# A first layer norm left out and block turns taken off TensorE, in a two-stage token kernel

## The chip, the cores and the metric

One core of a Trainium2 chip runs the whole kernel. The metric is the time of one execution on the device in microseconds; the median of 3 runs is shown. A core has TensorE (PE), VectorE (DVE), ScalarE (ACT), GpSimd (POOL) and SyncE (SP), each with its own instruction stream; they wait for each other by semaphores. DMAs are issued by SyncE here, and at the start by GpSimd too.

## What is computed

```python
# x: 8192 tokens of 512; all matrices are 512x512, all numbers float32
weights = AB/sqrt(512) * exp(W @ (ab*G).T - 0.5*|W|^2 * ab^2)     # random features of the weights
feats   = AB/sqrt(512) * exp(x @ (ab*G).T - 0.5*|x|^2 * ab^2)     # and of the tokens
x = layernorm(x + feats @ weights.T)                              # first norm
real, imag = x @ cos(theta + theta_noise), x @ sin(phi + phi_noise)
x = layernorm(x + sqrt(real**2 + imag**2))                        # second norm
```

## The kernel before

The tokens are worked in NB = 16 blocks of B = 512, each as C = 4 tiles of 128 tokens. Products are in float32 split into a rounded part (`_hi`) and a rest (`_lo`): three matmuls of 128x128 by 512 columns for each.

A block b goes through these steps on TensorE: the mix of features with weights (L813 to L815, 48 matmuls, into `token_ps[0..3]`), the projection of block b + 2 (L761 to L763, 48 matmuls, four results), the turns (L824: each tile of 128x512 as 4 transposes of 128x128 against the identity, into `turn_ps`), and the second stage. That is plain for blocks 0 and 1 (`PLAIN` = 2) and from block 2 on one level of a Winograd scheme: the tiles are taken in two pairs, a pair's turned features are halves, seven products M1 to M7 of six matmuls each are made (L910 to L912), and VectorE joins them (`join_u` and so on, L1375 to L1405). The order is M1, M6, M7, M5, M2, M4, M3. M1 needs only a first half, M6 needs the half sums.

Around it, for each tile: VectorE adds x to the mix (`residual1`, L1138), takes its statistics (L1109, L1113), GpSimd makes 1/sqrt(var + eps) and -mean times it (`scale1`, L377 to L393, four instructions on one column), ScalarE applies the first norm (`norm1`, L646), TensorE turns the tile, ScalarE rounds the turned tile out of PSUM (L651, L656, L657), VectorE makes the rest (L1015) and the half sums (L1354 to L1359), ScalarE rounds those (L661) and VectorE makes their rest (L1015). After the products ScalarE squares the joined tiles (L671), GpSimd adds the two squares of a pair (`pair_sum`, L398), ScalarE takes the root (L586), GpSimd or VectorE adds the residual (L402, L1334), VectorE takes the statistics (L1164), GpSimd the scales (`pair_scale2`, L408 to L414), ScalarE applies the second norm (`norm2`, L592) and SyncE stores a tile (L264). The norm of a block's last pair runs inside the next block's step.

For the block after next VectorE makes the exponents out of the projection's banks (L1020, `project_ps`, two banks used in turn), ScalarE the features (L503, L504), VectorE their rest (L1015); ScalarE rounds the turned input xT (L531) and VectorE splits it (`split_columns`, L1015, two instructions of 128x1024). The tokens' norms go through ScalarE (L462), a VectorE transpose (L1101), DRAM and back (L249, L253).

Each engine's order is written out by hand; each works strictly in that order, also SyncE, so that a wait in it holds up all DMAs behind it. The start makes cosine and sine on GpSimd, VectorE and ScalarE and waits for them in places. The last block has an order of its own.

## Time and profile before

| | us |
|---|---|
| median of 3 runs (lowest, highest) | 727.46 (727.32, 727.57) |
| the profiled execution, whole | 727.33 |
| its span in the profile | 725.5 |
| TensorE busy | 708.5 |
| VectorE busy | 563.8 |
| ScalarE busy | 489.7 |
| GpSimd busy | 279.2 |

Times of rows are microseconds from the start of the span; "busy" leaves out waits and the issue of DMAs. In a row of the timeline the first number is the start, the second the length, and the brackets at the end tell how long the engine had stood idle and what released it.

### The profile page before, as it was taken

What the parts mean: (1) busy time and instruction counts of PE and PEld (TensorE: products, weight loads), DVE (VectorE), ACT (ScalarE), POOL (GpSimd) and SP (SyncE); (2) the same over time, 40 slices, a digit from 0 to 9 for tenths busy, and PEclk for the clock granted to TensorE, in tenths of its full rate; (3) what the DMA queues carried; (4) which work ended last, traced back from release to release, by engine and by line L of the source; (5) the groups of instructions that cost most, each with busy time, mean ns of one, the idle gap of its engine ahead of it and who ended that gap; (6) DMA issues with size and microseconds to landing.
All of it is one profiled execution on the core that took longest, in us unless ns stands there. A gap on an engine that the chain in (4) does not pass through costs nothing.

```text
span 725.5 us, 10937 instructions
## 1 busy us (share of the span) xinstructions
PE 708.5 (98%) x3228; PEld 582.8 (80%) x3228; DVE 563.8 (78%) x963; ACT 489.7 (68%) x760; POOL 279.2 (38%) x465
## 2 busy tenths in 40 slices
PE   8999999999999999999999999999999999999993
PEld 7876788888888888888888888888888888888872
DVE  5799789797777868778786877869687777877686
ACT  7746757584957769395775939677594867757463
POOL 5765026606144250614416062341605235160525
PEclk9999999999999999999999999999999999999998
DMA  8761032310403232050322205032130503200011
GB/s 301 221 136 54 15 115 69 122 59 27 162 15 118 70 106 67 15 173 15 116 72 81 92 15 173 15 116 72 61 113 15 171 17 116 70 32 29 1 58 58
DMA packets 32753, 60.80 MB, mean 84 GB/s; under 512 B 3168, under 2 KB 3168, under 8 KB 32736
## 3 DMA queue, kind: packets, MB, share of 16 engines
q1 hardware_dynamic: 31584, 58.50, 24.3%
q0 software_dynamic: 1152, 2.10, 1.7%
q8 instruction: 8, 0.13, 0.1%
q14 instruction: 9, 0.07, 0.0%
HBM read 43.78 MB, written 16.81 MB: 84 GB/s over the span
## 4 chain that ended last, share of the span: by engine, by line
PE 90%; DVE 5%; ACT 2%; POOL 1%; issue 1%; POOLq 0%; ACTq 0%; DVEq 0%
PE token_ps L910 9%; PE token_ps L912 9%; PE token_ps L911 9%; PE token_ps L815 8%; PE token_ps L813 8%; PE token_ps L814 7%; PE project_ps L763 7%; PE project_ps L761 7%; PE project_ps L762 7%; PE turn_ps L824 4%; PE project_ps L910 3%; PE project_ps L912 3%; PE project_ps L911 3%; PE token_ps L843 1%; PE token_ps L841 1%; PE token_ps L842 1%
## 5 line engine op out<-in xcount | busy, mean ns | idle before, releaser
L398 POOL TENSOR_TENSOR late<-late 128x1024 f32<-128x1024 f32 x29 | 71.6, 2470 | 306.7 <-ACT late L671 306.7
L761 PE MATMUL project_ps<-xT_hi,gs_hi 128*128 128x512 f32 x248 | 100.1, 404 | 0.0
L813 PE MATMUL token_ps<-W_hi,F_hi 128*128 128x512 f32 x256 | 99.7, 389 | 0.0
L815 PE MATMUL token_ps<-W_hi,F_lo 128*128 128x512 f32 x256 | 99.6, 389 | 0.0
L814 PE MATMUL token_ps<-W_lo,F_hi 128*128 128x512 f32 x256 | 99.6, 389 | 0.0
L763 PE MATMUL project_ps<-xT_hi,gs_lo 128*128 128x512 f32 x248 | 97.1, 392 | 0.0
L762 PE MATMUL project_ps<-xT_lo,gs_hi 128*128 128x512 f32 x248 | 96.7, 390 | 0.0
L586 ACT ACTIVATE late<-late 128x1024 f32<-128x1024 f32 x29 | 30.8, 1062 | 77.1 <-POOL late L398 77.1
L671 ACT ACTIVATE late<-late 128x1024 f32<-128x1024 f32 x54 | 57.2, 1059 | 33.1 <-DVE late L1400 28.8
L646 ACT ACTIVATE z<-z,shift,rstd 128x512 f32<-128x512 f32 x56 | 45.2, 808 | 40.0 <-POOL shift L393 40.0
L1138 DVE TENSOR_TENSOR z<-token_ps,x_tok 128x512 f32<-128x512 f32 x64 | 44.1, 689 | 30.9 <-PE token_ps L815 27.6
L910 PE MATMUL token_ps<-T_hi,zT_hi 128*128 128x512 f32 x168 | 65.6, 390 | 0.0
L912 PE MATMUL token_ps<-T_hi,zT_lo 128*128 128x512 f32 x168 | 65.4, 389 | 0.0
L911 PE MATMUL token_ps<-T_lo,zT_hi 128*128 128x512 f32 x168 | 65.4, 389 | 0.0
L1015 DVE TENSOR_TENSOR zT_lo<-turn_ps,zT_hi 128x512 fp32r<-128x512 f32 x64 | 35.2, 568 | 33.1 <-ACT zT_hi L651 27.4
L1020 DVE SCALAR_TENSOR_TENSOR expo<-norm_bc,neg_half_ab,project_ps 128x512 f32<-128x512 f32 x62 | 46.0, 742 | 17.8 <-PE project_ps L763 16.0
L814 PEld LDWEIGHTS token_ps<-W_lo,F_hi 128*128 128x128 f32 x256 | 48.1, 188 | 10.0
L815 PEld LDWEIGHTS token_ps<-W_hi,F_lo 128*128 128x128 f32 x256 | 48.0, 188 | 10.0
L813 PEld LDWEIGHTS token_ps<-W_hi,F_hi 128*128 128x128 f32 x256 | 48.0, 188 | 9.9
L763 PEld LDWEIGHTS project_ps<-xT_hi,gs_lo 128*128 128x128 f32 x248 | 46.5, 188 | 10.2
L762 PEld LDWEIGHTS project_ps<-xT_lo,gs_hi 128*128 128x128 f32 x248 | 46.7, 188 | 9.1 <-issue 0.2
L761 PEld LDWEIGHTS project_ps<-xT_hi,gs_hi 128*128 128x128 f32 x248 | 46.6, 188 | 9.2 <-DVE xT_lo L1015 0.2
(214 smaller groups left out, 1802.7 us busy)
## 6 DMA issues: line engine op xcount, KB each, us to landing
x_tok<-in_x SPq DMA_DIRECT2D x16, 1024.0 KB, 5.6
out_tokens<-o_tile SPq DMA_DIRECT2D x62, 256.0 KB, 2.2
plain_xT_lo<-in_xT SPq DMA_DIRECT2D x14, 1024.0 KB, 5.3
norm_bc<-token_norms SPq DMA_DIRECT2D x15, 256.0 KB, 3.0
plain_T_hi<-in_gsT SPq DMA_DIRECT2D x4, 256.0 KB, 4.3
z<-in_wT SPq DMA_DIRECT2D x4, 256.0 KB, 4.6
plain_T_lo<-in_xT SPq DMA_DIRECT2D x1, 1024.0 KB, 7.9
plain_T_hi<-in_theta SPq DMA_DIRECT2D x4, 256.0 KB, 6.5
```

The costliest lines, as they stand in the source:

```text
L398: pool.tensor_tensor(parts[:, p, :, 0, :], parts[:, p, :, 0, :], parts[:, p, :, 1, :], ALU.add).then_inc(sum_made, 2)
L671: nc.scalar.activation(parts[:, p, i, :, :], parts[:, p, i, :, :], ACT.Square).then_inc(square_done, 2)
L761: nc.tensor.matmul(o, gs_hi[:, c, cols], rhs_hi[:, c, :], start=(c == 0), stop=False)
L762: nc.tensor.matmul(o, gs_hi[:, c, cols], rhs_lo[:, c, :], start=False, stop=False)
L763: return nc.tensor.matmul(o, gs_lo[:, c, cols], rhs_hi[:, c, :], start=False, stop=(c == C - 1))
L813: nc.tensor.matmul(o, F_hi[:, c, cols], W_hi[:, c, :], start=(c == 0), stop=False)
L814: nc.tensor.matmul(o, F_hi[:, c, cols], W_lo[:, c, :], start=False, stop=False)
L815: return nc.tensor.matmul(o, F_lo[:, c, cols], W_hi[:, c, :], start=False, stop=(c == C - 1))
L910: nc.tensor.matmul(o, left[0][i], right[0][i], start=(i == 0), stop=False)
L911: nc.tensor.matmul(o, left[0][i], right[1][i], start=False, stop=False)
L912: last = nc.tensor.matmul(o, left[1][i], right[0][i], start=False, stop=(i == H - 1))
L1020: stt(out=expo[:, to, :], in0=norm_bc[:, k, :], scalar=neg_half_ab[:, j:j + 1], in1=bank[:, :], op0=ALU.mult, op1=ALU.add).then_inc(expo_m ...
```

## The change

From block 1 on the first norm is left out. What it did is put elsewhere: the mean over features is taken out by subtracting from each row of cos and sin its column's mean (once, in the second block's step), and the scale by adding to the second norm's variance `damp` = eps * (var + eps) in place of eps. The residual that goes on is z without its norm.

From block 2 to 14 TensorE doesn't turn tiles. VectorE transposes a pair (128x1024) in squares of 32x32, SyncE stores it in 4 DMAs to DRAM in runs of 32 numbers (128 B) and fetches it in 3 DMAs (256, 128 and 128 KB, in runs of 128 numbers) to where the halves are wanted in SBUF. The half sums and rounding read that. The freed banks `turn_ps` take projections 2 and 3, so the projections wait for no exponent. The splits of xT go from VectorE to GpSimd. The last block keeps TensorE's turns, of the tiles without norm.

```diff
@@ build(), tensors
+    turned_dram = [nc.dram_tensor(f"turned_pair_{p}", (2 * D, P), F32, kind="Internal").ap() for p in range(2)]
-        parts = late.rearrange("p (q i t) d -> p q i t d", q=2, i=2)
+        parts = late.rearrange("p (q t i) d -> p q i t d", q=2, i=2)
+        turned_squares = [late[:, 4 * p + 2:4 * p + 4] for p in range(2)]
+        chunk_sums = [late[:, 0:2], late[:, 2:4]]
+        column_means = [late[:, 1, :], late[:, 3, :]]
@@ SyncE
+            def store_squares(b, p):
+                sp.wait_ge(squares_turned, 2 * (b - PLAIN) + p + 1)
+                rows = turned_dram[p].rearrange("(k r) (a t) -> a r k t", r=32, t=32)
+                for a in range(P // 32):
+                    src = turned_squares[p][32 * a:32 * a + 32].rearrange("r i (k t) -> r (i k) t", t=32)
+                    sp.dma_start(rows[a], src).then_inc(squares_stored[p], 16)
+            def fetch_halves(b, p):
+                sp.wait_ge(squares_stored[p], 64 * (b - PLAIN + 1))
+                first, second = turned_dram[p].rearrange("(i c q) n -> i q c n", i=2, q=P)
+                place = lambda lo, hi: zT_raw[:, p, lo * Q:hi * Q].rearrange("q (c n) -> q c n", n=P)
+                sp.dma_start(place(0, 2), first).then_inc(halves_landed[p], 16)
+                sp.dma_start(place(6, 7), second[:, 0:H]).then_inc(halves_landed[p], 16)
+                sp.dma_start(place(2, 3), second[:, H:C]).then_inc(halves_landed[p], 16)
...
                 if not first:
                     store_out(b - 1, 0)
                     store_out(b - 1, 1)
+                if moved:
+                    store_squares(b, 0)
+                    fetch_halves(b, 0)
+                    store_squares(b, 1)
+                if not first:
+                    store_out(b - 1, 2)
+                    store_out(b - 1, 3)
                 if ahead:
                     sp.wait_ge(y_made, C * (b + 1))
                     sp.dma_start(x_tok[:, slot], x_blocks[b + 2]).then_inc(x_loaded[slot], 16)
-                if not first:
-                    store_out(b - 1, 2)
-                    store_out(b - 1, 3)
+                if moved:
+                    fetch_halves(b, 1)
@@ GpSimd
-            def scale1(b, j):
...
+            def sum_chunks(k, raw):
+                pool.wait_ge(sine_made, 4 * C)
+                pool.tensor_tensor(chunk_sums[k], raw[:, 0:H, :], raw[:, H:C, :], ALU.add).then_inc(chunk_sums_made, 1)
...
+            def centre(k, raw, parts_made):
+                pool.wait_ge(parts_made, C)
+                pool.wait_ge(mean_copied, k + 1)
+                for c in range(C):
+                    pool.tensor_tensor(raw[:, c, :], raw[:, c, :], column_means[k], ALU.subtract).then_inc(centred, 1)
...
+            def step(b, ahead):
                 pair_sum(b - 1, 1)
-                scale1(b, 0)
                 pair_scale2(b - 1, 0)
-                scale1(b, 1)
                 pair_scale2(b - 1, 1)
-                scale1(b, 2)
-                scale1(b, 3)
+                make_damp(b)
+                if ahead:
+                    split_columns(b + 2, 0)
+                    split_columns(b + 2, 1)
                 pair_sum(b, 0)
                 pair_residual2(b, 0)
@@ ScalarE, step of a block
-                def norm1(j):
...
+                def round_halves(p):
+                    act.wait_ge(halves_landed[p], 48 * (s + 1))
+                    nc.scalar.activation(zT_hi[:, p, 0:3 * Q], zT_raw[:, p, 0:3 * Q], ACT.Copy).then_inc(halves_hi_made, 1)
@@ TensorE
+                    if j < 2:
+                        pe.wait_ge(chunk_sums_made, 2 * (j + 1))
+                        nc.tensor.matmul(turn_ps[j][:, :], ones[:, :], chunk_sums[j][:, 0, :],
+                                         start=True, stop=True).then_inc(mean_done, 1)
...
                     for j in range(C):
-                        pe.wait_ge(expo_made, C * (b + 2) + j - 1)
-                        project(j, project_ps[j % 2])
-                        if j < 2:
-                            turn(b, j)
-                    turn(b, 2)
-                    turn(b, 3)
+                        project(j, wide_project_ps[j])
@@ VectorE
+                def turn_squares(p):
+                    both = slice(2 * p, 2 * p + 2)
+                    dve.wait_ge(y_made, C * b + 2 * p + 2)
+                    nc.vector.transpose(turned_squares[p], z[:, both, :]).then_inc(squares_turned, 1)
+                def split_halves(p):
+                    dve.wait_ge(halves_hi_made, 2 * s + p + 1)
+                    dve.wait_ge(half_sums_made, 8 * s + 4 * p + 4)
+                    lower(zT_lo[:, p, 0:3 * Q], zT_raw[:, p, 0:3 * Q], zT_hi[:, p, 0:3 * Q]).then_inc(halves_lo_made, 1)
...
                 residual1(b, slot, 1)
+                moments1(0)
                 if more:
+                    turn_squares(0)
+                    pair_residual2(b - 1, 1)
...
+                    residual1(b, slot, 3)
+                    moments1(1)
+                    turn_squares(1)
...
+                    next_exponent(b, slot, 1, wide_project_ps)
+                    landed_half_sums(0)
+                    split_halves(0)
+                    next_exponent(b, slot, 2, wide_project_ps)
+                    split_half_sums(0)
+                    split_feature_pair(C * (b + 2) + 1, 0)
+                    next_exponent(b, slot, 3, wide_project_ps)
+                    landed_half_sums(1)
+                    join_u(0)
+                    split_halves(1)
+                    join_v(0)
+                    join_c22(0)
+                    join_w(0)
+                    join_c11(0)
+                    split_half_sums(1)
```

Not shown: in the second block's step ScalarE copies the two means (`copy_mean`) and rounds the centred matrices in four instructions (`round_centred`), VectorE makes the rests in four (`split_centred`), and its four first norms go. `make_damp` is two GpSimd instructions on 4 columns. `landed_half_sums` waits for the three fetches and makes the four half sums from SBUF. On ScalarE two of the four sums of squares of x stand later in the order than before.

## Rows read from the trace of the kernel before

**Rows 1.** The page: busy by engine, the chain by engine, the hardware DMA queue

```profile
PE 708.5 (98%) x3228; PEld 582.8 (80%) x3228; DVE 563.8 (78%) x963; ACT 489.7 (68%) x760; POOL 279.2 (38%) x465
...
PE 90%; DVE 5%; ACT 2%; POOL 1%; issue 1%; POOLq 0%; ACTq 0%; DVEq 0%
...
q1 hardware_dynamic: 31584, 58.50, 24.3%
```

**Rows 2.** Windows: stretch, length, busy by engine, TensorE's clock, DMA share; block 5

```profile
254.00:296.69 42.69, 42.69 (x197) 35.40 (x196) 33.16 (x58) 29.95 (x47) 14.81 (x28) 1.00 0.24 80
```

**Rows 3.** Timeline of TensorE, block 5: its first matmul and its first projection

```profile
254.03 0.39 PE L813 MATMUL token_ps<-W_hi,F_hi 128*128 128x512 f32 x1
...
264.91 0.39 PE L761 MATMUL project_ps<-xT_hi,gs_hi 128*128 128x512 f32 x1
```

**Rows 4.** The chain in order of time: start, length; the turns of tile 0

```profile
225.14 0.44 PE turn_ps L824 x4
...
267.80 0.44 PE turn_ps L824 x4
```

**Rows 5.** Timeline of VectorE, block 5: the residual of tile 1

```profile
259.67 0.69 DVE L1138 TENSOR_TENSOR z<-token_ps,x_tok 128x512 f32<-128x512 f32 x1 [1.30 <-PE token_ps L815]
```

**Rows 6.** Groups by line and shape, VectorE: busy us, mean ns, then idle before

```profile
L1101 DVE STREAM_TRANSPOSE norm_row<-norm_col 128x32 f32<-128x32 f32 x15 | 3.0, 200 | 2.0 <-ACT unused L462 2.0
...
L1044 DVE TENSOR_SCALAR neg_half_ab<-ab 128x4 f32<-128x4 f32 x1 | 0.2, 161 | 0.0
```

**Rows 7.** Timelines of ScalarE and GpSimd, blocks 5, 6; SyncE's stores by duration ns

```profile
264.26 1.52 ACT L592 ACTIVATE o_tile<-late,shift,rstd 128x512 f32<-128x512 f32 x2 [0.68 <-POOL shift L414]
...
262.69 0.20 POOL L408 TENSOR_TENSOR var_eps<-mv,eps 128x2 f32<-128x2 f32 x1
...
298.92 2.41 POOL L398 TENSOR_TENSOR late<-late 128x1024 f32<-128x1024 f32 x1 [1.76 <-ACT late L671]
...
L264 SPq DMA_DIRECT2D out_tokens<-o_tile x62: 332/333/378, 110.9 to 721.7; - x62
```

**Rows 8.** DMA: the stretch 289 to 290.9 (first line), then 8 to 9 us

```profile
q1 hardware_dynamic: 32, 0.00, 1.0%
...
DMA packets 557, 0.26 MB, mean 264 GB/s; under 512 B 429, under 2 KB 429, under 8 KB 557
...
q1 hardware_dynamic: 557, 0.26, 98.9%
```

**Rows 9.** Waits of SyncE: us in total, times, longest

```profile
SPq L253 <- DMA token_norms<-norm_row: 13.7, 15, 2.6
```

**Rows 10.** The page, DMA issues: KB each, us to landing

```profile
x_tok<-in_x SPq DMA_DIRECT2D x16, 1024.0 KB, 5.6
...
norm_bc<-token_norms SPq DMA_DIRECT2D x15, 256.0 KB, 3.0
```

**Rows 11.** Timelines of VectorE and ScalarE, block 5: half sums, their rounding and split

```profile
272.74 0.41 DVE L1354 TENSOR_TENSOR plain_zT_lo<-turn_ps,plain_zT_lo 128x256 f32<-128x256 f32 x1
...
274.31 1.06 ACT L661 ACTIVATE zT_hi<-plain_zT_lo 128x1024 fp32r<-128x1024 f32 x1
...
275.40 1.23 DVE L1015 TENSOR_TENSOR zT_lo<-plain_zT_lo,zT_hi 128x1024 fp32r<-128x1024 f32 x1 [0.41 <-ACT zT_hi L661]
```

**Rows 12.** Start: a sum over partitions in the chain; VectorE and TensorE near 75

```profile
16.34 0.86 PE turn_ps L793 x2
...
73.55 0.69 DVE L1015 TENSOR_TENSOR F_lo<-plain_F_lo,F_hi 128x512 fp32r<-128x512 f32 x1 [1.96 <-ACT plain_F_lo L504]
...
75.04 0.47 PE L841 MATMUL project_ps<-zT_hi 128*128 128x512 f32 x1 [1.67 <-DVE expo L1020]
```

**Rows 13.** Timelines of VectorE and GpSimd near 125: both with SBUF inputs

```profile
124.28 4.55 DVE L1015 TENSOR_TENSOR xT_lo<-plain_xT_lo,xT_hi 128x1024 fp32r<-128x1024 f32 x2
...
127.70 3.39 POOL L398 TENSOR_TENSOR late<-late 128x1024 f32<-128x1024 f32 x1
```

**Rows 14.** The chain in order of time, last block: a first norm

```profile
697.16 0.81 ACT z L646
```

254 lines of the change are left out of this document (141 added, 113 removed).

## The prediction

> **What bounds the kernel now.** I read the page's busy shares and its chain of work first: TensorE is busy for 708.5 of 725.5 us, and the chain that ended last lies on it for 90% of the span [rows 1]. Then the windows by block: in the 42.69 us of one block TensorE is busy throughout, VectorE for 33.2, ScalarE for 30.0, GpSimd for 14.8, at a full granted clock [rows 2]. Nobody else's work sets the length; only what TensorE has to do does. The reader should see that a microsecond taken from TensorE in a block is a microsecond of the span, until something else is later than it. For the rest I count time from a block's first mix matmul, at 254.03 us for block 5 [rows 3].
>
> **What goes from TensorE.** A 512-wide matmul follows the last after (264.91 - 254.03)/48 = 0.2267 us [rows 3]. A block has 48 for the mix, 48 to project and 14 products of 6, so 180: 40.81 us. From turn to turn a block takes 267.80 - 225.14 = 42.66, and 42.67 over two blocks, so its 16 turns (in 4 groups of 4) and the slower matmuls behind them cost 1.86 us. As a lower bound, the turns' own pieces in the chain are 4 x 0.44 = 1.76 us [rows 4]. Turns go from blocks 2 to 14, 13 of them: 13 x 1.86 = 24.2 us (22.9 by the lower bound). A block becomes 40.8 us: projections end at 13.6, 16.3, 19.0 and 21.8, the first product M1 starts at 21.8, M6 at 23.1, the second pair's M1 at 31.3.
>
> **Whether the turned halves come in time, first pair.** They are now made off TensorE, and this is the whole question. Tile 1's residual starts at 259.67, 5.64 after the block's start, as its mix allows, takes 0.69, and with the small moments behind it VectorE is free at 6.4 [rows 5]. The turn of 128x1024 has no row. The nearest is a turn of 128x32 at 200 ns, beside 161 ns for an operation on 4 columns: at least 1 ns and at most 43/32 = 1.34 ns a column, so 1.1 to 1.5 us [rows 6]. I take 1.3: squares ready at 7.7.
> SyncE must have issued the two stores of finished tiles before them. In block 5 these could go only behind ScalarE's second norms, which started at 264.26 (10.2), released by GpSimd, whose scales for them began at 262.69, behind the scales of this block's first norm [rows 7]. These waited for this block's first moments. They go. The sum of squares of the last pair ends 4.6 after a block's start (298.92 + 2.41 against 296.69) and from the second norms' scales to the norms it is 1.6 us more, so ScalarE's two norms lie at 6.2 to 7.7 and SyncE is free at about 8.1 [rows 7]. Four issues at 0.33 us each follow [rows 7].
> The stores write 4096 runs of 128 B a pair. Cost of one: 32 small packets took 1.0% of 16 engines in 1.9 us, 9.5 ns each. In a full queue, 557 packets in 1 us at 98.9% of 16 engines, 128 of them large, leave 7.6 ns for each of 429 small ones, with 98 ns for a large one (24.3% of 16 x 725.5 us over some 28,400 of them) [rows 1, 8]. So 4096 take 1.9 to 2.4 us on 16 engines if they come as fast as that; if they come at the 429 a microsecond of that window, 9.5 us. I take 3.0, near the lower end, since that window's engines were busy with large packets. SyncE waited 13.7/15 = 0.9 us after its last small store [rows 9]. Stored at 8.1 + 1.3 + 3.0 + 0.9 = 13.3. The three fetches are 0.5 MB: between 3.0 us for 256 KB and 5.6 for 1 MB, so 3.9 [rows 10]. They land at 17.2.
> The need: from the first half sum at 272.74 over ScalarE's rounding to the split's end at 276.63 it is 3.9 us, and M6 wants that at 23.1: landing by 19.2 [rows 11]. Slack 2.0 us. VectorE asks only at 17.2 anyhow, behind exponent 1, which needs the projection that ends at 16.3.
>
> **Second pair.** Its squares are ready at 13.5, its stores are issued behind the first fetch, at 14.4 to 15.7, and done at about 19; the tile stores and the 1 MB of x are in the queue ahead of its fetch, which lands by 23 to 24.5. What is queued behind VectorE's wait for it is join U to C11 of the first pair, 5.5 us in all with sums and split, and the second M1 needs C11 at 31.3: landing by 25.8. Slack 1.3 to 2.8 us. Also behind it on SyncE is xT's load, due when projection 3 is done at 21.8; it lands by 28.5, and nobody needs its splits before 40.8 + 10.9.
>
> **What else moves.** VectorE a block: gone are two splits of xT (2 x 1.15) and four splits from PSUM (2 x 1.0); new are two turns (2.6) and two splits of 768 columns (1.8). It stays near 33 of 40.8 us. ScalarE loses four first norms and two roundings of three pieces, 4.2 us net. Nothing there bounds. GpSimd loses four scales, some 5.8 us, and gets xT's splits, two instructions of the size that takes it 2.4 to 2.5 us [rows 7]. In its order they stand ahead of the first pair's sum, due at about 35.6; xT is rounded by 32, so the splits end at 36 to 37. That sum may be 1.4 us late, and VectorE's first work of the next block with it. I charge nothing, and up to 0.6 us a block in the range. The wider banks take the expo waits off the projections; TensorE had no idle there, so no gain.
>
> **Start and end.** Two sums over partitions with the ones matrix are new on TensorE; one of the same kind and size is 0.86 us of the chain now, so 1.7 us for both [rows 12]. GpSimd's sums of chunks start when the last sine is out, near 71, 3.8 us for each matrix by the 2.4 us of one of 1024 columns, and end near 79 to 80; TensorE asks at 83.3, so that wait costs nothing, nor does the chain of centring and splitting, whose last split (VectorE, about 109.6) just precedes its use at 110. But they run beside VectorE's splits of features, the first at 73.55, and TensorE waited 1.7 us at 75.04 for the exponent behind them [rows 12]. Where VectorE's splits from two SBUF tensors met GpSimd's sum, two took 4.55 us, against 1.23 for one in rows 11 [rows 13]. I charge 1.4 us (0 to 3). VectorE then enters block 2 later by some 1.3 us and its pair may land late: 0.5 us once.
> In the last block TensorE waited for a first norm, 0.81 us of ScalarE in the chain: 0.7 us back [rows 14].
> The Trainium skill (SBUF — State Buffer, Who interferes with whom) says that a VectorE instruction with two SBUF inputs and a GpSimd one that reads SBUF exclude each other for a whole instruction. The 4.55 us agree. By that rule alone the start would cost up to one GpSimd instruction, 2.5 us, in place of 1.4, and the splits of xT beside splits of features as much in a block, where both have slack.
>
> **Sum.** 725.5 - 24.2 + 1.7 + 1.4 + 0.5 - 0.7 = 704.2 us of span. The profiled execution took 727.33, 1.8 more than its span: 706.0. It is 0.1 below the median of 727.46.
>
> **The rivals.** *All hidden* (0.60): 706, with 702 to 710 for the bounds above. *Partly late* (0.15): the halves land 1 us after 19.2, or GpSimd's sum pushes each block by as much: 706 + 13 = 719. For it: slacks of 2 us made of six estimated steps. *Stores too slow* (0.20): slower. The 4096 small runs take 6.2 us a pair, the middle between 3.0 and 9.5. The first pair lands at 20.4, 1.2 late. The second's stores are done near 25, its fetch lands at 29.5 in place of 25.8 + 1.2, 2.5 late; 3.7 x 13 = 48 us on 706 gives 754. It decides from 1.64 us of loss a block, (727.46 - 706)/13, a store of about 5.2 us. For it: nothing in this trace stores more than four small runs at a time. Against it: the 429 small ones in 1 us came in a queue that was full.
> The Trainium skill (DMA: Bandwidth & Descriptors, Specifications) names 512 B as the least run for the full rate and says that smaller ones are read, modified and written. No run here shows it; by that page the stores would be this last case.
> *The gain is eaten up to nothing, or the turns' work isn't on the path as I read it* (0.05): 727. That TensorE is never idle in a block [rows 2] speaks against the second.
>
> **Range and chances.** 702 to 730 leaves out the 0.20 of slow stores less a little that falls below 730. Some 0.2% (1.5 us) is what a measurement of this kernel can tell from no change. Faster 0.75, same 0.05, slower 0.20.
>
> **What would show it.** Right: blocks of 40.8 us with TensorE busy throughout; no L824 from block 2 to 14; SyncE's first fetch near 13 and its landing near 17 after a block's start; second norms from 6.2. Stores too slow: VectorE's half sums or TensorE's M1 or M6 waiting for the fetch, and blocks over 42.7. A turn much over 1.5 us, or SyncE's issues much over 0.33 us each, would break the schedule first.

## The result, and the profile after

| | before | after |
|---|---|---|
| median (lowest, highest), us | 727.49 (727.32, 727.57), 4 runs | 765.46 (763.25, 767.61), 4 runs |
| ratio to before, 95% interval | 1 | 1.0517 (1.0497 to 1.0538) |
| span of the profiled execution | 725.5 | 762.9 |

The change makes the kernel 5.2% slower; 706.0 was predicted, and 702 to 730 as the range. The page of the changed kernel, busy time by engine, the chain by engine, the hardware DMA queue (it answers to [rows 1]):

```profile
PE 709.7 (93%) x3024; PEld 576.2 (76%) x3024; DVE 599.0 (79%) x939; ACT 446.9 (59%) x658; POOL 304.6 (40%) x299
...
q1 hardware_dynamic: 167616, 85.77, 41.7%
...
PE 32%; DVE 18%; DMA 18%; issue 9%; SPq 9%; POOL 7%; ACT 5%; DVEq 0%; POOLq 0%; ACTq 0%
```

TensorE has 204 instructions less and yet is busy for 1.2 us more, in a span 37.4 us longer. The chain lay on it for 90% and now does for 32%; the rest goes through VectorE, DMAs and SyncE. Block 8, from its first mix matmul at 405.66 to the next block's at 451.72, and stretches in it (columns as in [rows 2]):

```profile
405.66:451.72 46.06, 42.73 (x181) 34.88 (x180) 35.30 (x56) 26.77 (x40) 16.43 (x15) 0.96 0.47 120
437.00:439.00 2.00, 0.10 (x1) 0.00 (x0) 1.97 (x3) 1.97 (x4) 0.00 (x0) 1.00 0.00 0
441.00:443.00 2.00, 2.00 (x7) 1.59 (x6) 2.00 (x2) 1.11 (x3) 2.00 (x1) 0.61 0.00 0
443.00:445.00 2.00, 2.00 (x6) 1.55 (x6) 2.00 (x2) 0.00 (x0) 2.00 (x2) 0.53 0.00 0
```

A block was 42.66 us and was to be 40.8. By the starts of the blocks in TensorE's timeline, blocks 2 to 13 take 677.8 - 130.2 = 547.6 us, 45.63 each; block 14 takes 40.8. So the 37.4 us are: 4.2 until block 2 starts (130.2 for 126.02), 12 x (45.63 - 42.67) = 35.5, less 1.9 in block 14 and some 0.4 at the end. What block 8 takes above 40.8 us, 5.26, is two things. TensorE stands idle from 437.1 to 440.4, which puts the next matmul 3.5 us late. Then its granted clock, 1.00 in the first of the three stretches of 2 us, is 0.61 and 0.53 in the other two, near the lower of its two levels (1.2 GHz): the 12 matmuls behind the wait take 4.46 us and not 2.72, 1.7 us more. The waits in it, VectorE's (first two lines) and TensorE's timelines of block 8:

```profile
434.84 0.42 DVE L1447 TENSOR_TENSOR plain_zT_lo<-plain_zT_lo 128x256 f32<-128x256 f32 x1 [5.34 <-DMA plain_zT_lo<-turned_pair]
...
439.70 0.68 DVE L1505 TENSOR_TENSOR late<-token_ps,late 128x512 f32<-128x512 f32 x1
```

```profile
440.44 0.50 PE L1003 MATMUL token_ps<-cos_hi,zT_hi 128*128 128x512 f32 x1 [3.33 <-DVE late L1505]
...
444.06 0.63 PE L1004 MATMUL token_ps<-T_lo,zT_hi 128*128 128x512 f32 x1
```

TensorE's second M1 waits for join C11 (L1505), which stands on VectorE behind the wait for the second pair's halves. Over the kernel that is 12 waits of TensorE, 33.1 us, and VectorE's wait for landed halves is 62.7 us. What led to it, SyncE's timeline of block 8 (issue of DMAs):

```profile
414.88 2.39 SPq L291 DMA_DIRECT2D turned_pair<-late  x4
419.64 0.38 SPq L298 DMA_DIRECT2D plain_zT_lo<-turned_pair  x1
...
421.20 2.70 SPq L291 DMA_DIRECT2D turned_pair<-late  x4
424.19 1.14 SPq L283 DMA_DIRECT2D out_tokens<-o_tile  x2
425.61 0.41 SPq L335 DMA_DIRECT2D x_tok<-in_x  x1
426.40 0.38 SPq L298 DMA_DIRECT2D plain_zT_lo<-turned_pair  x1
426.83 0.51 SPq L299 DMA_DIRECT2D plain_zT_lo<-turned_pair  x1
427.38 1.14 SPq L300 DMA_DIRECT2D plain_zT_lo<-turned_pair  x1
428.78 0.47 SPq L340 DMA_DIRECT2D plain_xT_lo<-in_xT  x1
```

The chain in order of time has the last of the three DMAs of this fetch at 427.38, and its landing 7.44 us later. From the first issue, 426.40, it is 8.4 us; over the 12 blocks 7.8 on average, where the first pair's fetch takes 3.9 to 4.0.

```profile
427.38 7.44 DMA plain_zT_lo<-turned_pair
```

And a window of the landing: in 428.70 to 435.00 the 16 DMA engines are full (1.03) at 328 GB/s.

```profile
428.70:435.00 6.30, 6.30 (x30) 5.21 (x29) 0.96 (x3) 1.99 (x4) 0.00 (x0) 1.00 1.03 328
```

In that queue stand 0.5 MB of output tiles and 1 MB of x ahead of the fetch, and 1 MB of xT behind it; the window counts them all, so by itself it doesn't tell which of them hold the fetch (run 5 does). One more thing is new, on VectorE and GpSimd right behind that wait:

```profile
441.43 3.40 DVE L1107 TENSOR_TENSOR F_lo<-plain_F_lo,F_hi 128x1024 fp32r<-128x1024 f32 x1
```

```profile
440.70 6.39 POOL L493 TENSOR_TENSOR xT_lo<-plain_xT_lo,xT_hi 128x1024 fp32r<-128x1024 f32 x2 [18.33 <-ACT xT_hi L596]
```

VectorE's split of features, 1.2 us elsewhere, takes 3.40 beside GpSimd's two splits of xT, which take 6.39 together.

### The profile page after: what moved, and what is told of

It reads as the page before. It is cut to its first block, busy times and chain, and to the rows that moved or that the text cites. A ratio compares the mean times of both kernels' runs of the same rounds, so it can differ in the third digit from the quotient of the medians.

```text
span 762.9 us, 10262 instructions
## 1 busy us (share of the span) xinstructions
PE 709.7 (93%) x3024; PEld 576.2 (76%) x3024; DVE 599.0 (79%) x939; ACT 446.9 (59%) x658; POOL 304.6 (40%) x299
## 3 DMA queue, kind: packets, MB, share of 16 engines
q1 hardware_dynamic: 167616, 85.77, 41.7%
## 4 chain that ended last, share of the span: by engine, by line
PE 32%; DVE 18%; DMA 18%; issue 9%; SPq 9%; POOL 7%; ACT 5%; DVEq 0%; POOLq 0%; ACTq 0%
DMA plain_zT_lo<-turned_pair 9%; DMA turned_pair<-late 8%; SPq L291 5%; PE token_ps L1003 4%; PE token_ps L1004 4%; PE token_ps L1005 4%; POOL late L451 3%; DVE F_lo L1107 2%; PE token_ps L897 2%; PE token_ps L895 2%; PE token_ps L896 2%; DVE zT_lo L1107 2%; ACT late L759 2%; DVE late L1497 2%; SPq L299 1%
## 5 line engine op out<-in xcount | busy, mean ns | idle before, releaser
L493 POOL TENSOR_TENSOR xT_lo<-plain_xT_lo,xT_hi 128x1024 fp32r<-128x1024 f32 x24 | 76.7, 3214 | 214.7 <-ACT xT_hi L596 214.7
L1003 PE MATMUL token_ps<-cos_hi,zT_hi 128*128 128x512 f32 x112 | 48.5, 433 | 36.1 <-DVE late L1505 33.1
L657 ACT ACTIVATE o_tile<-late,shift,rstd 128x512 f32<-128x512 f32 x58 | 44.2, 809 | 54.9 <-POOL shift L468 54.9
L1107 DVE TENSOR_TENSOR F_lo<-plain_F_lo,F_hi 128x1024 fp32r<-128x1024 f32 (+1 forms) x38 | 70.2, 1851 | 2.7 <-ACT plain_F_lo L569 2.5
L568 ACT ACTIVATE F_hi<-expo,ab 128x512 fp32r<-128x512 f32 x64 | 46.1, 720 | 40.1 <-DVE expo L1112 40.0
L1447 DVE TENSOR_TENSOR plain_zT_lo<-plain_zT_lo 128x256 f32<-128x256 f32 x26 | 11.0, 425 | 62.7 <-DMA plain_zT_lo<-turned_pair 62.7
L1107 DVE TENSOR_TENSOR zT_lo<-plain_zT_lo,zT_hi 128x1024 fp32r<-128x1024 f32 (+1 forms) x54 | 58.9, 1090 | 1.7 <-ACT zT_hi L749 1.1
L1003 PEld LDWEIGHTS token_ps<-cos_hi,zT_hi 128*128 128x128 f32 x112 | 22.2, 198 | 47.2 <-DVE late L1505 34.2
L843 PE MATMUL project_ps<-xT_hi,gs_hi 128*128 128x512 f32 x144 | 57.0, 396 | 0.0
L845 PE MATMUL project_ps<-xT_hi,gs_lo 128*128 128x512 f32 x144 | 56.1, 390 | 0.0
L844 PE MATMUL project_ps<-xT_lo,gs_hi 128*128 128x512 f32 x144 | 56.1, 389 | 0.0
L1256 DVE BATCH_NORM_STATS2 stats<-late 128x6 f32<-128x512 f32 x58 | 38.8, 689 | 21.9 <-POOL late L455 21.4
```

The lines of the kernel that those rows point to most:

```text
L493: pool.tensor_tensor(xT_lo[:, both, :], xT_raw[:, both, :], xT_hi[:, both, :].bitcast(F32), ALU.subtract).then_inc(xT_lo_made, H)
L843: nc.tensor.matmul(o, gs_hi[:, c, cols], rhs_hi[:, c, :], start=(c == 0), stop=False)
L844: nc.tensor.matmul(o, gs_hi[:, c, cols], rhs_lo[:, c, :], start=False, stop=False)
L1003: nc.tensor.matmul(o, left[0][i], right[0][i], start=(i == 0), stop=False)
L1107: return tt(dst, whole, hi.bitcast(F32), ALU.subtract)
```

## The experiments

The theory, **Q**: the second pair's fetch lands late because it shares the DMA engines with the load of x ahead of it and that of xT behind it. The rivals: **O**, only VectorE's order is at fault (it waits for the fetch with the joins behind); and **S**, the prediction's own rival, the stores in runs of 128 B are too slow. Each kernel was timed against the kernel before on the same chip (727.6 to 727.9 us).

**1. The fetch ahead (Q).**

```diff
                 if moved:
                     store_squares(b, 0)
                     fetch_halves(b, 0)
                     store_squares(b, 1)
+                    fetch_halves(b, 1)
                 if not first:
                     store_out(b - 1, 2)
                     store_out(b - 1, 3)
                 if ahead:
                     ...
-                if moved:
-                    fetch_halves(b, 1)
```

> Base: the changed kernel at 765 us, blocks of 45.6 us. Edit: SyncE issues the second pair's three fetches before the two tile stores and the 1 MB load of x, with nothing else moved. Theory Q (the fetch is late because it shares the DMA engines with the 1 MB of x ahead of it and the 1 MB of xT behind it): it lands some 3 us after its last issue, as in block 14 which has no such loads (2.8 us), not 7.4; TensorE's gap before the second M1 goes and with it the halved clock behind it; blocks of 40.8 to 41.5 us, total 706 to 716. Theory O (VectorE's order alone: the wait for the fetch ahead of the joins): the same gain, as the wait ends early. Theory S (the stores of 128-byte runs are the bound): the fetch still can't start before its stores are in, so only 1 us a block, 750 or more.

Measured 732.30 us, ratio 1.0067 (1.0048 to 1.0085), 33 us less than the change but 16 us above the range that Q gave. The fetch isn't issued earlier: from 21.9 us after the block's start in the block looked at, against 20.7. But it lands 4.0 us after its first issue in place of 7.8, at 25.9, as the prediction needed it. The waits for C11 are all but gone (0.4 us once), and in the list of TensorE's waits a smaller one stands in their place:

```profile
PE token_ps L1002 <- ACT late L754: 16.9, 12, 2.1
```

L754 is ScalarE's copy of the second pair's M1. ScalarE's timeline of one block has it behind the rounding of xT, that behind xT's landing, and TensorE behind it:

```profile
292.38 2.01 ACT L595 ACTIVATE xT_hi<-plain_xT_lo 128x1024 fp32r<-128x1024 f32 x2 [1.88 <-DMA plain_xT_lo<-in_xT]
...
294.91 1.04 ACT L758 ACTIVATE late<-late 128x1024 f32<-128x1024 f32 x1
295.85 0.57 ACT L754 ACTIVATE late<-token_ps 128x512 f32<-128x512 f32 x1
```

**2. The joins ahead (O).** join_u(0) to join_c11(0) go ahead of landed_half_sums(1) and split_halves(1) on VectorE; the fetch stays late.

> Edit on the changed kernel: VectorE makes join U to C11 of the first pair before it waits for the second fetch; the DMAs stay as they are. Theory O: the second M1 then waits for the halves' split alone, some 2.5 us after the landing in place of 5.6; the gap of TensorE shrinks from 2.8 us to under 1 and its clock isn't halved; 765 - 12 x (2.3 + 1.9) = 715. Theory Q alone: the fetch is as late as before and M1 and M6 of the second pair still wait for it; M1 1 us and M6 up to 1 us, 12 x 2 on 706: 725 to 735. Theory S: like Q.

Measured 735.56, ratio 1.0108 (1.0091 to 1.0125), at the upper end of Q's range and far from O's 715. It takes away nearly as much as run 1: the late fetch costs mostly through what is queued behind the wait for it. TensorE then waits for the split of the halves themselves, 15.5 us in all. Q and O aren't rivals but two halves of one cause, a late landing and VectorE's order; either half mended takes back 30 to 33 us.

**3. Long runs (S).** The stores go in runs of 4096 B; the turn of the squares is left out of the computation by that.

```diff
-                rows = turned_dram[p].rearrange("(k r) (a t) -> a r k t", r=32, t=32)
+                rows = turned_dram[p].rearrange("(a r m) n -> a r (m n)", a=4, r=32)
...
-                    src = turned_squares[p][32 * a:32 * a + 32].rearrange("r i (k t) -> r (i k) t", t=32)
+                    src = turned_squares[p][32 * a:32 * a + 32].rearrange("r i d -> r (i d)")
```

> Edit on the changed kernel: the four stores of a pair write the same bytes in runs of 4 KB in place of 128 B (the turned tiles then land in a wrong order in DRAM, so this leaves the turn out; its time is that of the same work otherwise). Theory S: the stores are the bound, the total falls to 710 to 720. Theory Q: the stores take 1 to 2 us less each pair, the second fetch is issued that much earlier but stays behind the x load and meets the xT load; it lands perhaps 1 us earlier; 745 to 760.

Measured 741.55, ratio 1.0199 (1.0182 to 1.0216): the small runs cost 24 us of the changed kernel, but without them it would still be slower than before. The issue of a store, from the views of the line L291 of the changed kernel and of this one (ns, least, median, most):

```profile
L291 SPq DMA_DIRECT2D turned_pair<-late x104: 345/622/1087, 140.7 to 694.7; - x104
```

```profile
L291 SPq DMA_DIRECT2D turned_pair<-late x104: 337/422/514, 139.1 to 668.4; - x104
```

They land 3.0 us after their issue with small runs and 2.4 with long ones. The second fetch goes out 1.4 us earlier for that and lands 1.5 us earlier (means of 12 blocks); it still takes 7.8 us. The queue's page line of this kernel has the same bytes in fewer packets and less of the engines' time:

```profile
q1 hardware_dynamic: 64448, 85.77, 36.0%
```

By it and the changed kernel's 41.7% of 762.9 us, the small runs take 52 us more of all 16 engines, an estimate of 2.0 us for each of the 26 pairs stored.

**4. The gap filled.** Eight matmuls of no use stand ahead of the second pair's products from block 2 to 14, behind a wait for the exponents.

> Edit on the changed kernel: 8 matmuls of 512 columns (1.8 us) whose result nobody uses, on TensorE between the first pair's last product and its wait for the second M1, in blocks 2 to 14. It measures the clock's part by itself. If the halved clock behind the gap (granted 0.53 to 0.61 for 3.8 us, 1.9 us lost a block) comes from the gap, most gaps shrink under 1.5 us, the clock stays and the total is 765 - 12 x 1.9 + 2 = 744. If the clock falls for another reason, 765 to 768.

Measured 765.29 with a clock of 0.995 in place of 0.968: the clock was kept, and nothing was won. A block is 45.4 us: 40.8, 1.8 of filling, waits of 1.2 for C11 and 1.0 for ScalarE's copy, and 0.6 that the list of waits doesn't show. The slow stretch had covered that second wait. The miss is mine; a clock that falls in a wait costs less than the slow matmuls add up to, if something else is late right behind.

**5. xT held back.** SyncE waits for the second pair's landing before it issues the load of xT.

> The changed kernel, but SyncE waits for the landing of the second pair's halves before it issues the 1 MB load of xT; the 1 MB of x stays ahead of the fetch. In the changed kernel that fetch lands 7.4 us after its last issue, in the run that put it ahead of both loads 2.7 us. If the xT load behind it is what slows it: it lands within 4 to 5 us of its issue, VectorE's wait for it shrinks from 5.3 to some 2.5 us, TensorE's wait for C11 from 3.1 to about 0.5, and the block is 42 to 43 (725 to 735 us), unless the later xT holds something else. If it is the 1 MB of x ahead of it: it still lands 6 to 7 us after its issue, and the time is 765 or, with xT later still, up to 780.

Measured 753.69, ratio 1.0350 (1.0333 to 1.0367), 12 us less. But not by the fetch. (The 7.4 and 2.7 us in the expectation don't compare: the one is from the start of the last issue, the other from its end; here it is from the start of the first.) SyncE's first issue and VectorE's wait in one block are 8.2 us apart, and over the 12 blocks it is 7.8 us, as in the changed kernel.

```profile
422.93 0.39 SPq L298 DMA_DIRECT2D plain_zT_lo<-turned_pair  x1
```

```profile
431.09 0.43 DVE L1448 TENSOR_TENSOR plain_zT_lo<-plain_zT_lo 128x256 f32<-128x256 f32 x1 [4.92 <-DMA plain_zT_lo<-turned_pair]
```

The load of xT behind the fetch costs it nothing; what is ahead of it, the tile stores and x, costs it all of the 3.8 us. The window that answers to the full one of the changed kernel, from 2.3 us behind the fetch's first issue to its landing, has less in it and is no shorter for that, so the 1.03 there was in part xT's own traffic:

```profile
425.23:431.09 5.86, 5.86 (x28) 4.85 (x27) 0.95 (x2) 1.82 (x3) 0.00 (x0) 1.00 0.71 212
```

What was won is elsewhere: xT is later, so GpSimd's splits start behind VectorE's split of the features and not beside it. Groups by line, first of the changed kernel, then of this one (busy us, mean ns):

```profile
L1107 DVE TENSOR_TENSOR F_lo<-plain_F_lo,F_hi 128x1024 fp32r<-128x1024 f32 (+1 forms) x38 | 70.2, 1851 | 2.7 <-ACT plain_F_lo L569 2.5
```

```profile
L1108 DVE TENSOR_TENSOR F_lo<-plain_F_lo,F_hi 128x1024 fp32r<-128x1024 f32 (+1 forms) x38 | 43.4, 1143 | 3.0 <-ACT plain_F_lo L570 3.0
```

Theory Q, which named both loads, falls by half: the traffic ahead counts, the load behind doesn't. And there is a third cause, call it **G**, GpSimd's splits of xT.

**6 to 8. ScalarE's copy, first attempts.** The wait for the copy was to go by moving square_tile(0, 1) and copy_first(1) ahead of ScalarE's wait for xT and the rounding of xT: once with the fetch ahead, once in the changed kernel, once with the filling too.

```diff
+                    square_tile(0, 1)
+                    copy_first(1)
                     if ahead:
                         act.wait_ge(xT_loaded, 16 * (b + 3))
                         round_columns(0)
                         round_columns(1)
                         sum_square(b + 3, 1, slot, 1 - slot)
-                    square_tile(0, 1)
-                    copy_first(1)
                     square_tile(0, 0)
```

> The second pair's fetch goes out right behind its stores (as in the run that did only that, 732.3 us), and ScalarE copies the second pair's M1 (copy_first) and squares tile pair (0,1) ahead of its wait for the next-but-one block's xT load, not behind it and behind the rounding of xT. Theory Q as it now stands (the load on the DMA engines is the first loss, and what is left in that run, a wait of 1.3 to 2.1 us a block of M2 for that copy, is ScalarE's order behind a late xT load): the wait goes, 12 blocks by 1.5 us = 18 us less, 714 us, blocks of 41.3 or less. Theory O (VectorE's order is the bound): the joins are still behind the second fetch, so 730 to 734. Theory S (the stores themselves are too slow): a wait on the landed halves stays, 725 or more.

> The changed kernel with only ScalarE's reordering of the run above: copy_first of the second pair and square_tile(0,1) ahead of the wait for xT; the second fetch stays where the change put it. Theory Q: the copy was in time in the changed kernel (ready at 447.1, needed at 447.6 us), so nothing or little is won, 760 to 766 us. If the copy is what holds the blocks, some 740.

> The run above with eight matmuls of no use (1.8 us) set in the gap of 3.1 us ahead of the second pair's first wait on C11, so that TensorE isn't idle long enough to lose its clock. The run with the eight matmuls alone took 765.29 us at a clock of 0.995, though in the changed kernel 12 matmuls behind the gap take 4.46 us and not 2.72. If what took that gain back was the copy behind the xT rounding: the 1.74 us a block come back now, 12 by 1.74 = 21 us, 744 us. If the gain was taken by something else (VectorE, the fetch): 760 to 766 again.

Measured 746.02 (ratio 1.0241, 1.0218 to 1.0264), 792.98 and 795.62: all three are misses, 14 to 30 us slower than the kernels they start from. The wait for the copy did go. But the rounding of xT is later, so GpSimd's splits of xT are, and behind them in its order the sum of squares and the residual of the first pair. VectorE's next block opens with the statistics of that (first kernel, GpSimd, then VectorE):

```profile
432.51 4.78 POOL L492 TENSOR_TENSOR xT_lo<-plain_xT_lo,xT_hi 128x1024 fp32r<-128x1024 f32 x2 [19.43 <-ACT xT_hi L595]
437.23 2.41 POOL L450 TENSOR_TENSOR late<-late 128x1024 f32<-128x1024 f32 x1
440.94 2.40 POOL L454 TENSOR_TENSOR late<-z,late 128x1024 f32<-128x1024 f32 x1 [1.30 <-ACT late L650]
```

```profile
443.37 1.29 DVE L1256 BATCH_NORM_STATS2 stats<-late 128x6 f32<-128x512 f32 x2 [4.79 <-POOL late L454]
```

VectorE stands idle for 4.8 us there, so its turn, the stores and the first fetch do, and TensorE waits for the split of the first pair's half sums (25.4 us, 14 times). In the second kernel, with the late fetch, the squares are ready at 8.9 to 10.1 us where the changed kernel has mostly 7.6 to 7.9, and the wait for C11 takes 46.0 us in all and not 33.1. The block's front has little slack (1.5 us for the first pair's landing in the changed kernel) for anything that is late at the end of the last one.

**9. The splits of xT on VectorE.** They are taken from GpSimd and put behind turn_norms (9a, with 6's order), behind VectorE's last join (9b, the changed kernel otherwise), or there with the fetch ahead and both of the first pair's squares ahead of xT's rounding (9c; 9d has long stores beside, the turn left out).

> The first of these four with the splits of xT taken from GpSimd and put back on VectorE, behind its turn of the norms and ahead of its last two joins, as 2 more VectorE operations of 1.2 us each. If GpSimd's two subtractions (3.2 us each) still hold a block by the lock on the shared port: 2 to 8 us less than the first of these four, near 706. If they are hidden there: the same, within 0.3%. If VectorE is short of time at the block's end: a wait for C21 or C12 at the next block's first projection, and up to 2 us a block more (735).

> The changed kernel with one part undone: the splits of xT are VectorE's again, behind its last join of the block; fetches, stores and ScalarE's order as the change has them. If the second fetch among the loads of x and xT is the main loss and GpSimd's splits a lesser one (3.2 us each for 2.4 and VectorE's split of the features beside them 3.4 for 1.2): the wait for C11 stays, 750 to 765 us. If GpSimd's splits were the main loss: under 735.

> Second fetch right behind its stores; ScalarE copies the second pair's M1 and squares both tiles of the first pair ahead of its wait for xT and the rounding of xT; the splits of xT go from GpSimd to VectorE, behind its last join of the block. So GpSimd sums the first pair's squares some 5 us earlier, and the statistics that open VectorE's next block don't wait for it. In the run with the copy alone moved ahead (746 us) VectorE waited 5.7 us at a block's start for that, and the first pair's halves came 2.5 us late; with the splits on VectorE (732.6 us) 1.1 and 1.3 us. If TensorE's 180 matmuls and no third wait are left: blocks of 40.8 to 41.5, 707 to 714 us, faster than the kernel before. If the first pair's way through DRAM (stored 13.3, lands 17.7 of 19.2 us at best) is itself too slow: a wait for its half sums of over 1 us stays, 722 to 735.

> e11's order, with the stores of the squares in runs of 4096 bytes and not of 128 (the turn is left out of the computation by that; bytes, issues and fetches are the same). Theory S (small runs hold the turn back even in the better order): over 5 us faster than e11. Theory Q: the stores are hidden there, within 3 us of e11.

Measured 732.61, 777.96, 758.55 and 742.50; 9b and 9c are 13 and 24 us above the highest that was expected of them, and 9a wins 13 us on run 6 but doesn't come near 706. The first pair's halves are late again in 9a and 9c (1.3 and mostly 1.6 to 3.4 us a block): VectorE's two splits at the block's seam take 5.2 us in 9c, since GpSimd's residual and sum of squares run beside them, and hold its next block up by as much. In 9b the splits stand at the same seam, and the first squares are ready at 11.3 us in four of the blocks 3 to 13 and at 8.0 in the others.

```profile
355.93 5.23 DVE L1103 TENSOR_TENSOR xT_lo<-plain_xT_lo,xT_hi 128x1024 fp32r<-128x1024 f32 x2
```

9d is 16 us faster than 9c, over the 5 that S asked for: where the turn is late, the small runs do count.

**10. The part undone at its old place.** The splits stand between the joins of the two pairs, where the kernel before has them; in the changed kernel (10a) and with the fetch ahead (10b).

```diff
                     join_c12(0)
+                    if ahead:
+                        split_columns(b + 2, 0)
+                        split_columns(b + 2, 1)
                     join_u(1)
```

> The changed kernel with one part undone, the splits of xT on VectorE at the place where the kernel before has them (between the joins of the two pairs); nothing else. In the run with the splits at the block's end they cost more (778 us), since VectorE opens the next block 3 us later there. Loads among the fetch as the main loss: the wait for C11 of some 3.3 us stays, 755 to 770 us. GpSimd's splits as the main loss: 735 or less.

> The run with only the second fetch moved ahead of tile stores and x (732.3 us), and beside it the splits of xT on VectorE between the joins of the two pairs. That run's blocks are 42.9 long with a wait of 1.3 to 2.0 us at +38.6 for ScalarE's copy of M1, which stands behind a square that waits for xT's rounding. GpSimd's share: if its splits only delay the sum of squares and the next block's start, 728 to 733; if they hold the copy too: 710 to 720.

Measured 754.09 (1.0336, 1.0288 to 1.0384) and 723.88 (0.9946, 0.9929 to 0.9963). 10a lies 1 us below its range, 10b between its two. By the medians G is 11 us of the change (run 5 won 12) and 8 us with the fetch ahead. The size in the change is rough: 10a's runs spread from 749 to 759 us, and the profiled executions differ by 6.4 us only, 1.8 of it ahead of block 2.

G isn't one mechanism. In the change the collision with VectorE's split of the features is part of it. With the fetch ahead there is no collision left to undo; groups by line of run 1's kernel:

```profile
L492 POOL TENSOR_TENSOR xT_lo<-plain_xT_lo,xT_hi 128x1024 fp32r<-128x1024 f32 x24 | 56.8, 2389 | 219.2 <-ACT xT_hi L595 219.2
L1106 DVE TENSOR_TENSOR F_lo<-plain_F_lo,F_hi 128x1024 fp32r<-128x1024 f32 (+1 forms) x38 | 43.3, 1142 | 3.0 <-ACT plain_F_lo L568 3.0
```

What the splits cost there lies, by the dates, in GpSimd's order: they end at 40.4 to 40.7 us of a block, the first pair's sum of squares and residual come behind them, and VectorE has its first squares at 8.7 us of the next block and not at 7.9 as in 10b.

**11. The orders put right.** SyncE and ScalarE as below; 11a has the splits of xT on VectorE as in 10, 11b leaves them on GpSimd, as the change has them.

```diff
@@ SyncE
+                if moved:
+                    store_squares(b, 0)
                 if not first:
                     store_out(b - 1, 0)
                     store_out(b - 1, 1)
                 if moved:
-                    store_squares(b, 0)
                     fetch_halves(b, 0)
                     store_squares(b, 1)
+                    fetch_halves(b, 1)
+                if ahead:
+                    sp.wait_ge(project_done, C * (b + 3))
+                    sp.dma_start(xT_raw[:, :, :], xT_blocks[b + 2]).then_inc(xT_loaded, 16)
                 if not first:
                     store_out(b - 1, 2)
                     store_out(b - 1, 3)
...
@@ ScalarE
                     if ahead:
-                        act.wait_ge(x_loaded[slot], 16 * (pair + 2))
-                        sum_square(b + 3, 0, slot, 1 - slot)
                         act.wait_ge(xT_loaded, 16 * (b + 3))
                         round_columns(0)
                         round_columns(1)
-                        sum_square(b + 3, 1, slot, 1 - slot)
                     square_tile(0, 1)
                     copy_first(1)
                     square_tile(0, 0)
                     if ahead:
+                        act.wait_ge(x_loaded[slot], 16 * (pair + 2))
+                        sum_square(b + 3, 0, slot, 1 - slot)
+                        sum_square(b + 3, 1, slot, 1 - slot)
```

> A version of the change with four orders made again. SyncE: the first pair's squares are stored ahead of the tile stores of pair 0 of the block before, the second pair's fetch comes right behind its stores, then the load of xT, then tile stores 2 and 3, then x. ScalarE: xT rounded first, then the squares of the first pair and the copy, the sums of squares last. VectorE: the splits of xT between the last join of the first pair and the first join of the second, where its trace shows idle time, GpSimd does none. If the turn through DRAM itself is fast enough and only orders were at fault (first pair's halves in some 17 us from the block's start, second pair's 25, matmuls at 21.8 and 31): blocks of 40.8 to 41.5, 706 to 714 us, faster than the kernel before. If the store-and-fetch round trips are the bound whatever the order (theory S): a wait for landed halves stays and the time is 725 to 740.

> The version above with the splits of xT left on GpSimd, where the change has them. If GpSimd's two splits (4.7 to 6.4 us for both) still hold the first pair's sum of squares and with it the statistics at the next block's start, and VectorE by the shared lock: 1 to 2.5 us a block more than above, 12 to 30 us. If they are hidden: within 3 us of it.

Measured 706.26 (ratio 0.9706, 0.9689 to 0.9722) and 706.40 (0.9706, 0.9690 to 0.9723): both are 3% faster than the kernel before. In 11a blocks 3 to 14 take 40.80 us each. In 11b TensorE is busy all through block 7 at full clock (windows: the block, and the stretch in which the second fetch lands), and SyncE's timeline shows the order:

```profile
333.44:374.25 40.81, 40.81 (x182) 33.80 (x181) 35.36 (x57) 26.39 (x39) 16.43 (x15) 1.00 0.52 135
352.50:356.70 4.20, 4.20 (x20) 3.50 (x19) 4.20 (x6) 2.40 (x4) 0.00 (x0) 1.00 0.44 130
```

```profile
341.17 2.25 SPq L291 DMA_DIRECT2D turned_pair<-late  x4
343.68 1.02 SPq L283 DMA_DIRECT2D out_tokens<-o_tile  x2
345.60 0.38 SPq L298 DMA_DIRECT2D plain_zT_lo<-turned_pair  x1
...
347.16 2.85 SPq L291 DMA_DIRECT2D turned_pair<-late  x4
352.51 0.38 SPq L298 DMA_DIRECT2D plain_zT_lo<-turned_pair  x1
...
355.54 0.38 SPq L334 DMA_DIRECT2D plain_xT_lo<-in_xT  x1
```

The same bytes in the same packets as in the changed kernel (queue q1 has 167616 packets and 85.77 MB in both) go by a DMA share of 0.44, not 1.03, while the second fetch is under way. GpSimd's splits make no difference here, though they still take up to 6.39 us and VectorE's split beside them 3.42: xT is rounded at 30.7 us of the block and the splits end at 36.2, in block 8 of the change at 35.8 and 41.4.

**12. Which queue.** 12a has ScalarE's new order alone, 12b SyncE's alone.

> The changed kernel (765 us), SyncE's order as the change has it, with ScalarE's order alone of the run that took 706.4 us: xT rounded first, then the squares of the first pair and the copy, the sums of squares of x last. If SyncE's order is the cause and ScalarE's only the second wait behind it: the fetch still lands some 7 us after its issue, the wait for C11 of about 3 us stays, 750 to 768 us. If ScalarE's order is what counts: under 735.

> The changed kernel with SyncE's order alone of the run that took 706.4 us (first pair's squares stored ahead of the tile stores, second fetch right behind its stores, then xT, tile stores 2 and 3, x); ScalarE and GpSimd as the change has them. ScalarE there begins with a sum of squares that waits for x, which is now loaded last, and the rounding of xT and the copy of M1 stand behind it. If SyncE's order is the cause of all: 706 to 710. If ScalarE's is a cause of its own: a wait of 1 to 3 us a block for the copy at some +38, 718 to 740 us.

Measured 791.41 (1.0890, 1.0864 to 1.0915), well over its range, and 723.44 (0.9946, 0.9929 to 0.9962). SyncE's order is worth 42 of the 59 us (33 by the place of the second fetch alone, run 1), ScalarE's the other 17, but only on top of it: alone it costs 26. There the fetch is as late as in the change, and the earlier rounding of xT brings GpSimd's splits beside two of VectorE's instead of one (timeline of VectorE in one block; 1.22 us each elsewhere):

```profile
402.40 3.25 DVE L1107 TENSOR_TENSOR zT_lo<-plain_zT_lo,zT_hi 128x1024 fp32r<-128x1024 f32 x1
405.57 3.38 DVE L1107 TENSOR_TENSOR F_lo<-plain_F_lo,F_hi 128x1024 fp32r<-128x1024 f32 x1
```

In 12b the copy of M1 is what is left, as expected: 13.2 us, 12 times. There ScalarE waits for x first.

## Why the prediction was wrong, step by step

*What bounds, and what TensorE is spared: right.* Without waits a block is 40.80 us, in block 14 of the changed kernel and in twelve blocks of 11a. The 706.0 us is what the change would take if all were hidden; 11b's span of 704.1 stands beside the predicted 704.2.

*First pair: right, with a slack smaller by 0.5.* From the start of block 8: squares ready at 7.9 (7.7 predicted; the turn takes 1.25 us for 1.3), ScalarE's norms from 7.0 (6.2), SyncE free at 9.1 (8.1). Issuing four stores took 2.4 us, not 1.3, 0.6 each; they are stored at 14.0 (13.3), and the fetch lands at 17.7 (17.2; needed by 19.2). Two terms missed in opposite ways: the issue took 1.1 us more, and from its end to "stored" it was 2.4 us where the sum had 3.0 + 0.9. So the issues of over 0.33 us, named as a sign that would break the schedule first, did come and didn't break it for this pair.

*Second pair: this is the step that failed.* "Lands by 23 to 24.5" was measured at 29.2 in block 8, 3.4 behind the 25.8 named as the need. 1.7 us of it is the stores, issued from 15.5 and stored at 20.7 (19; with the first pair's terms the prediction's own 15.7 would have led to 19.6). The rest, 3.0 us or more, is the fetch: the text named "the tile stores and the 1 MB of x" as being in the queue ahead of it, and gave it 4 to 5.5 us for all of that. The price was at hand: 3.0 us for 256 KB in [rows 10] is of a transfer by itself, and at the 264 GB/s of [rows 8] 1.5 MB ahead are an estimated 5 to 6 us of full engines. Measured: 4.0 us with nothing ahead, 7.8 behind the stores and x, 8.4 in block 8.

*What is queued behind VectorE's wait:* named rightly (joins U to C11), and run 2 shows it: with them ahead of the wait the time falls by 30 us. But the next lateness was not asked for. Behind C11 comes ScalarE's copy of M1; the prediction moved xT's landing to 28.5 (in run 1's kernel ScalarE still waits for it at 34.4) and followed it only to its splits, not through ScalarE's queue, where the copy stands behind its rounding. It costs 17 us once SyncE's order is right (12b against 11b).

*GpSimd's splits:* "I charge nothing, and up to 0.6 us a block". They cost some 11 us in the change (runs 5 and 10a, by the medians), up to 0.95 a block, 8 with the fetch ahead, and nothing in 11b. The dates were wrong first: xT was to be rounded by 32 and the splits to end at 36 to 37; in block 8 it was 35.8 and 41.4. The kernel before ends its rounding at 34.2 of block 5 already (timeline of ScalarE):

```profile
286.20 1.99 ACT L531 ACTIVATE xT_hi<-plain_xT_lo 128x1024 fp32r<-128x1024 f32 x2
```

The price of the collision was in [rows 13] (4.55 us for two) and was applied to the start only. The Trainium skill (SBUF — State Buffer, Who interferes with whom) says that a VectorE instruction with two SBUF inputs and a GpSimd one that reads SBUF contend; the trace agrees here: 3.40 us for VectorE's split in place of 1.22.

*The clock:* a term that the sum lacked. Behind block 8's wait of 3.3 us the granted clock is 0.61 to 0.53 and twelve matmuls take 1.7 us more. Run 4 shows that keeping it up (0.995 over the execution) alone wins nothing.

*The rival of slow stores (754):* its time was nearest, its mechanism was not the one at work. Its point of decision was 5.2 us for the small runs of a pair, in the term that had 3.0, with 0.9 of waiting behind it; from the end of the issue to "stored" block 8 has 2.4 us for both together, and with the orders of run 11 the same small runs are hidden whole. They do take part: 24 us in the changed kernel (run 3), by the slower issue and by the engines' time that they add to the queue, so that the second fetch goes out 1.4 us earlier without them. The Trainium skill (DMA: Bandwidth & Descriptors, Specifications) names 512 B as the least run for the full rate; the landing of 3.0 us for 2.4 and the 2.0 us a pair of engines' time fit with that as far as the rate goes; no run here shows the reading and modifying.

*Start and end:* 4.2 us until block 2 for 3.1 predicted with what VectorE adds there, and some 0.4 us back at the end for 0.7. In 11b block 2 starts at 128.94, 2.9 us later than before, and over the other kernels with the change it is 1.5 to 3.8, so the sum of the start's terms was about right, and a microsecond or more of the 4.2 varies from kernel to kernel.

What stays open: how the 3.8 us that the fetch loses split between the tile stores and x, since no run moved only one of them; how G divides into the collision and GpSimd's order in the change itself; and why a pair of reorderings adds up to more than its parts in 12, beyond the collision that the rows show.

## What to carry to other kernels

A transfer's time from a trace is that of its own neighbourhood: before a small transfer with a deadline is put into a queue, add up the bytes in flight ahead of it, and order the queue by deadline. Here that took 42 us off (12b), and with ScalarE's order as well 765 us became 706, without a byte or an operation less. When a step moves, follow each engine's queue past the first late thing to the second (here ScalarE's copy behind a rounding that waits for a load), and ask at each change of order what comes to lie beside what: the same reordering of ScalarE won 17 us with the loads in order and lost 26 without.

## What the runs showed of the hardware

- Four stores of 128 KB in 1024 runs of 128 B each: 622 ns to issue one (422 with runs of 4096 B, 332 for a tile's store in [rows 7]), 3.0 us to landing (2.4). The small runs take an estimated 2.0 us more of all 16 engines for each 0.5 MB (run 3).
- VectorE's turn of 128x1024 by squares of 32x32 takes 1.25 us, as long as an addition of that size (1.18).
- A fetch of 0.5 MB in three DMAs lands 4.0 us after its first issue with no other load or tile store ahead of it (run 1), 7.8 behind 1.5 MB of others; 1 MB issued right behind it on the same queue adds nothing (7.8 with it and without, run 5).
- A subtraction of 128x1024 from SBUF on VectorE is 1.2 us, 3.3 to 3.4 beside the same on GpSimd; GpSimd's own is 2.4 alone and 3.2 beside VectorE's.
